# A fused Perceiver layer in eight blocks: four token buffers in place of a store and reload of the residual, and another plan for the first block

## The reference

```python
def xattn(x, ctx):                       # ctx: 257 keys of 256 for each sequence
    q, k, v = x @ Wq.T + bq, ctx @ Wk.T + bk, ctx @ Wv.T + bv
    p = softmax((q @ k.T) / sqrt(256))
    return (x + p @ v) @ Wo.T + bo
def mixer(x):                            # inner width 512, 16 states
    h = conv3(x @ in_w.T + in_b)         # depthwise over the 32 tokens
    u = silu(h)
    d, Bm = (u @ x_proj_w.T + x_proj_b)[..., :64], (...)[..., 64:]
    delta = softplus(d @ dt_w.T + dt_b)
    s[t] = exp(delta[t] * A) * s[t-1] + delta[t] * u[t] * Bm[t]     # scan over t
    return (s.sum(-1) + u * D) @ out_w.T + out_b
def ffn(x):                              # weights ternary, activations to 8 bits
    return down(silu(gate(quant(x))) * up(quant(x)))
x = x + xattn(layernorm(x), ctx)
x = x + mixer(layernorm(x))
x = x + ffn(layernorm(x))
```

## Time and profile before

| | us |
|---|---|
| median of 3 runs (lowest, highest) | 1072.03 (1071.34, 1080.11) |
| the profiled execution, its own time | 1073.63 |
| its span (first to last instruction) | 1071.8 |
| busy: PE / DVE / POOL / ACT | 950.8 / 895.7 / 858.0 / 759.6 |

### The profile page before, as it was taken

The page is one execution under the profiler, slowest core; times in us unless marked ns, Lnnn a source line. Parts: engine busy times, 40 slices in busy tenths (PEclk is TensorE's granted clock), DMA queues, the critical chain, the costliest instruction groups (busy, mean ns, idle before and its releaser), DMA issues.

```text
span 1071.8 us, 13076 instructions
## 1 busy us (share of the span) xinstructions
PE 950.8 (89%) x4175; PEld 511.9 (48%) x4210; DVE 895.7 (84%) x1210; ACT 759.6 (71%) x1321; POOL 858.0 (80%) x617
## 2 busy tenths in 40 slices
PE   8786998899988998899898998899898998687886
PEld 7452443445445554545445554446354554432554
DVE  2434797899988999799988999799987999899955
ACT  2346558777797869777796869777896869765634
POOL 1357998998978898799978898799978898899900
PEclk9997999999999999999999999999998999989999
DMA  9813440435042520535042520544042400400000
GB/s 347 323 44 158 166 169 30 168 114 221 21 143 98 214 80 21 197 129 207 20 162 91 202 79 21 197 155 180 2 177 75 143 1 2 177 0 1 1 20 20
DMA packets 21483, 122.63 MB, mean 114 GB/s; under 512 B 3431, under 2 KB 4071, under 8 KB 8872
## 3 DMA queue, kind: packets, MB, share of 16 engines
q1 hardware_dynamic: 15800, 86.99, 22.3%
q10 hardware_dynamic: 5616, 34.81, 8.7%
HBM read 114.19 MB, written 7.60 MB: 114 GB/s over the span
## 4 chain that ended last, share of the span: by engine, by line
PE 35%; ACT 22%; DVE 20%; issue 10%; DMA 6%; POOL 5%; SPq 1%; ACTq 0%; DVEq 0%; POOLq 0%
PE bank L1014 17%; PE acc L1014 13%; DVE state L877 11%; ACT decay L665 6%; DMA out<-res 3%; POOL state L598 2%; ACT u L756 2%; ACT soft L651 2%; ACT L665 2%; ACT u L764 2%; DVE raw L860 2%; ACT hid L682 2%; DMA res<-x_scratch 1%; DVE hm L943 1%; DMA brep<-in_w_gateT 1%
## 5 line engine op out<-in xcount | busy, mean ns | idle before, releaser
L877 DVE TENSOR_TENSOR_SCAN state<-decay,state 128x512 f32<-128x512 f32 (+1 forms) x352 | 590.1, 1694 | 45.5 <-ACT decay L665 27.9
L598 POOL TENSOR_TENSOR state<-w,brep 128x512 f32<-128x512 f32 (+1 forms) x352 | 612.6, 1771 | 0.1
L1014 PE MATMUL acc<-state,ident 128*128 128x512 f32 x832 | 409.2, 608 | 16.4 <-DVE state L877 12.0
L665 ACT ACTIVATE decay<-delta,neg_a 128x496 f32<-128x496 f32 x512 | 329.5, 669 | 98.6 <-DVE state L877 97.2
L1014 PEld LDWEIGHTS acc<-state,ident 128*128 128x128 f32 x832 | 147.8, 192 | 166.0 <-issue 114.2
L606 POOL TENSOR_TENSOR state<-state 128x512 f32<-128x512 f32 x96 | 122.2, 1273 | 52.6 <-DVE state L877 51.3
L651 ACT ACTIVATE soft<-x_in,nmr,rstd 128x256 f32<-128x256 f32 x64 | 33.2, 589 | 48.9 <-POOL nmr L564 48.9
L1014 PE MATMUL bank<-xn_t,in_w 128*128 128x512 f32 x128 | 60.1, 603 | 7.5 <-DVE u L1006 5.7
L629 POOL TENSOR_TENSOR w<-delta,u 128x512 f32<-128x512 f32 x32 | 39.9, 1271 | 31.0 <-ACT delta L788 31.0
L692 ACT ACTIVATE sg<-bank,ag 128x512 f32<-128x512 f32 x64 | 43.6, 681 | 29.3 <-PE bank L1014 29.0
L1014 PE MATMUL bank<-out_w,u 128*128 128x256 f32 x256 | 58.0, 382 | 6.7 <-DVE u L868 6.7
(11 more groups left out here) (145 smaller groups left out, 1348.6 us busy)
## 6 DMA issues: line engine op xcount, KB each, us to landing
keys<-in_keys_t SPq DMA_DIRECT2D x32, 1028.0 KB, 4.8
keys<-in_keys_n SPq DMA_DIRECT2D x32, 1024.0 KB
brep<-b_scratch ACTq DMA_DIRECT2D x32, 1024.0 KB, 6.7
x_in<-in_x SPq DMA_DIRECT2D x7, 512.0 KB, 5.4
x_scratch<-x_in SPq DMA_DIRECT2D x6, 512.0 KB, 2.6
res<-x_scratch SPq DMA_DIRECT2D x6, 512.0 KB, 3.5
out<-res SPq DMA_DIRECT2D x6, 512.0 KB, 8.6
brep<-in_w_gateT SPq DMA_DIRECT2D x1, 1024.0 KB, 13.4
```

What stands on the lines that cost most here:

```text
L598: nc.gpsimd.tensor_tensor(state[g % CPT][:, 0:count, :], w[:, m, :].unsqueeze(1).to_broadcast((P, count, TOK)), brep[:, n:n + count, :], A ...
L665: last = nc.scalar.activation(decay[:, to + i, :, 1:LEN], d, ACT.Exp, scale=neg_a[:, m, n + i:n + i + 1])
L877: nc.vector.tensor_tensor_scan(flat, decay[:, of:of + count, :, :].rearrange("p c q l -> p (c q l)"), flat, 0.0, ALU.mult, ALU.add).then_i ...
L1014: return nc.tensor.matmul(o, l, r, start=first, stop=last)
```

## The change

- `x_in` has four buffers; block b lives in `x_in[b % 4]` until it is stored. `res`, `x1_scratch`, the store at L528, the load at L511 and their semaphores are gone. `x2`, `stats3`, `xn3` and `finish` use `x_in[b % 4]`. The load of block j+1 waits, from j = 3 on, for the store of block j-3.
- Loads of x and stores of out go in pairs of groups: two DMAs of 256 KB where there was one of 512 KB (the first load of x excepted).
- In block 0 the keys have six buffers: the three, and `u[1]`, `w` and `delta`, which are not in use yet. SP issues six key loads, then the mixer's weights, then the last two key loads (each after the score that frees its buffer), then the feed-forward weights, then the last key rows of groups 2 and 3.
- In block 0 attention alternates between banks D, E and A, B, so the score of group g waits for the exponential of group g-2, not g-1.
- Phase 0 has its own tables (`FIRST`, and another `PREPARE`), phase 1 too (`SECOND`). Phases 2 to 7 keep their order on every engine. In phases 8 and 9 a few entries swap places.
- `softplus0` comes ahead of the `b_load`s in phase 0, and `softplus1` ahead of `c0`.
- `SIZES` makes the block sizes a table; all are 4 groups, so tiles and instruction shapes stay as they were.

Orders in phase 0 after the change. DVE: `stats1, qk, vo_rep, s_max0, s_max1, s_neg0, s_bias0, s_neg1, mixer_weights, s_bias1, s_max2, s_neg2, s_max3, s_bias2, vo_evac, s_neg3, s_bias3, p_sum0-2, abs_sum0, abs_sum1, p_sum3, abs_sum2, abs_sum3, scales, x1, ...`. PE: `turn1, query, score0, score1, vo, score2, p_turn0, score3, attend0, p_turn1, attend1, z_turn0, p_turn2, z_turn1, p_turn3, attend2, attend3, z_turn2, total, z_turn3, attn_out, ...`. ACT: `xn1, evac1, q_evac, exp0, p_last0, exp1, p_evac0, p_last1, exp2, p_evac1, exp3, p_last2, mixer_weights, z_evac0, z_evac1, zt_evac0, p_evac2, zt_evac1, p_last3, p_evac3, z_evac2, z_evac3, zt_evac2, zt_evac3, ..., x_dbl, softplus0, b_load0-3, softplus1, c0`. POOL ends with `times_u0-3, c0, c1, c2`.

```diff
-KEY_LOADS = (("t", 0), ("t", 1), ("n", 0), ("t", 2), ("n", 1), ("t", 3), ("n", 2), ("n", 3))
+FIRST_KEYS = ((("t", 0), 0), (("t", 1), 1), (("n", 0), 3), (("t", 2), 2), (("n", 1), 4), (("n", 2), 5),
+              (("t", 3), 0), (("n", 3), 1))
...
-        x_in = [sb(f"x_in{i}", [P, GROUPS, DIM]) for i in range(2)]
-        res = sb("res", [P, GROUPS, DIM])
+        x_in = [sb(f"x_in{i}", [P, GROUPS, DIM]) for i in range(4)]
...
+        keys = [sb(f"keys{i}", [P, GSEQ * HALVES * KEYS]) for i in range(3)] + [
+            k[:, :, :].rearrange("p m t -> p (m t)") for k in (u[1], w, delta)]
...
+        def att_banks(g, scan):
+            return (D, E) if scan or g % 2 == 0 else (A, B)
...
-                if post and pre:
-                    reach(sp, out_stored, j - 2, 0)
-                    sp.dma_start(res[:, :, :], t["x1_scratch"][j - 2]).then_inc(res_loaded, 16)
                 if pre:
                     if not scan:
-                        for k in range(3):
-                            load_keys(j, k)
+                        for k in range(6):
+                            load_keys(0, k)
                         load_mixer_weights()
+                        for k in (6, 7):
+                            load_keys(0, k)
                         load_ffn_weights()
...
-                    if j < BLOCKS - 2:
-                        reach(sp, res_biased[1], j, 1)
-                        sp.dma_start(t["x1_scratch"][j], x_in[par][:, :, :]).then_inc(x1_stored, 16)
...
-                    sp.dma_start(out[j - 2], (res if pre else x_in[par])[:, :, :]).then_inc(out_stored, 16)
+                    for of, at, to in pairs(b):
+                        sp.dma_start(out[at][:, to, :], x_in[b % 4][:, of, :]).then_inc(out_stored, 16)
...
                     elif part == "x2":
                         reach(dve, mixed, b, g + 1)
-                        if g == 0 and pre:
-                            reach(dve, res_loaded, b, 16)
-                        if g == 0 and not pre:
+                        if g == 0:
                             reach(dve, res_biased[1], b, 1)
...
 # LAST (phase 9): among others
-    ("h_scale", [37, 42, 59, 65]),
+    ("h_scale", [37, 42, 59, 68]),
-    ("gate", [22, 24, 25, 37, 43, 46, 58, 60]),
+    ("gate", [22, 24, 25, 37, 43, 46, 61, 63]),
```

More of the change, by code:

```diff
@@ L17 @@
 SLOTS = TILES * CPT
+SIZES = (4,) * 8
+COUNT = len(SIZES)
+FIRST_GROUP = [sum(SIZES[:b]) for b in range(COUNT + 1)]
 BG = 4
@@ new lines @@
+POST = [
+    ("h_evac", [32, 35, 73, 79]),
+    ("down", [32, 60, 75, 82]),
+    ("y_last", [0]),
+    ("x_evac", [13]),
+    ("scale_x", [12]),
+    ("tanh", [14, 16, 19, 24, 41, 46, 58, 68]),
+    ("x_max", [9]),
+    ("out_proj", [2, 2]),
+    ("x2", [4, 5]),
+    ("h_turn", [29, 33, 72, 78]),
+    ("scale_h", [21, 33, 69, 75]),
+    ("h_max", [19, 31, 54, 71]),
+    ("x_turn", [7]),
+    ("stats3", [6]),
+    ("h_floor", [20, 31, 58, 72]),
+    ("gate", [15, 17, 19, 28, 43, 45, 57, 68]),
+    ("h_scale", [22, 32, 67, 73]),
+    ("hidden", [16, 18, 20, 30, 43, 50, 63, 69]),
+    ("up", [10, 14, 17, 23, 37, 44, 51, 65]),
+    ("rstd3", [4]),
+    ("xn3", [9]),
+    ("finish", [31, 63, 77, 86]),
+]
@@ L137 @@
 }
-PREPARE = [
-    ("qk", [2]),
-    ("total", [33]),
-    ("scales", [39]),
-    ("vo_evac", [23]),
-    ("mixer_weights", [23]),
-    ("quantise", [26, 48, 63, 67]),
-    ("abs_sum", [12, 16, 22, 38]),
-    ("vo", [5]),
-    ("vo_rep", [5]),
-]
 def _scan_slots():
```

705 lines of the change are left out of this document (462 added, 243 removed).

## The result

The kernel after takes 1048.4 us (median of 4 runs, 1047.18 to 1049.7), the kernel before in the same session 1071.7: ratio 0.9749, 95% interval [0.9715, 0.9782]. Of the profiled executions before took 1073.63 us (span 1071.8), after 1048.12 (span 1046.3), so the two traces differ by 25.5 us, which is what has to be placed. The kernel before ran again in four later sessions, with medians of 1074.1 to 1075.7 us, and the kernel after once more in the last of these, with 1047.94 for 1075.52, 27.6 us less. The ratio is computed from the single executions and is not the quotient of the medians, which is 0.9783 in the first session and 0.9744 in the last; the gain is 2.2 to 2.6% by all of them.

What follows compares the result with a forecast made beforehand. It took waits shared by PE, DVE and ACT, including the residual's round trip, as the bound, with POOL in phase 1. 11.0 + 1.7 + 0.3 + 1.45 + 0.5 + 0.4 = 15.4 us won gave 1056.5 us, range 1050 to 1066.

Steps and rivals of the forecast that it cites:

- Term 1: Phases 3 to 7: DVE's five waits for the residual's reload at `x2` go, 11.0 us won (9.5 to 11.6).
- That agreement is my reason to count nearly all of it: Phases 3 to 6 less their waits, 117.5 us each, match phase 2's 117.73, which had no such wait.
- Term 2: Block 0's attention: `attn_out` 1.7 us earlier, at 48.2 for 49.89, and 0.3 more up to `x_dbl`.
- The three new waits: Block 0: `mixer_weights` ahead of `s_bias1`, `score3` of `attend0`, `total` of the last `z_turn`; gain kept small, -5 to +1.
- Term 3: End of phase 0: first scan 0.9 us later relative to `x_dbl`, but POOL's `c3` 1.45 us earlier, counted as won.
- Term 4: Phase 1's new order: same instructions in other places, 0.5 us won; at most 6.8 won or 2.6 lost.
- Term 5: Phases 8 and 9: `h_scale2` ahead of `gate6` wins 0.7 us, the split last store costs 0.33; net 0.4 won.
- The estimate of 2.3 us more: Loads and stores in halves: 512 KB would take 2.3 us longer at 138 GB/s, making the sum 1058.5.
- What was to be seen: Profile after: no DMA wait at `x2`, phases 3 to 6 at 117.5 to 117.8, `attn_out` at 48, phase 1 106 to 108 us.
- The wait is given back: Rival, phases 3 to 7: PE might set the pace, so only 4.4 us remain, 1067.6 us; chance 0.08.
- The starved start: Rival, block 0: at 203 GB/s `attn_out` comes at about 63.9, PE runs at 1.2 GHz, 1087 us; chance 0.05.

Runs made afterwards that it cites:

- r1_kept: The kernel before with four buffers of tokens and no store and reload of the residual, old tables and start kept: 1056.24 us, ratio 0.9808.
- r2_traffic: The kernel before with four token buffers, the tokens' store and a DRAM-to-DRAM read still issued, no engine waiting for the read: 1057.49 us, ratio 0.9821.
- r9_old_table0: The kernel after with phase 0 ordered by the two tables of the kernel before, six key buffers and four attention banks kept: 1067.97 us, ratio 0.9938.
- r10_old_end0: The kernel after with four rows of its first table (softplus, times_u, b_load, dt) back at or near their old places: 1051.86 us, ratio 0.9786.
- r8_old_table1: The kernel after with phase 1 ordered by the table that the kernel before used in all phases: 1054.53 us, ratio 0.9807.
- r11: The kernel after with phases 8 and 9 ordered by the tables of the kernel before: 1049.32 us, ratio 0.9766.

## Why the prediction was right and wrong

**Term 1, the reload: right about the wait, without the clock behind it.** Forecast 11.0 (9.5 to 11.6). Measured: 18.0 in phases 3 to 7, all of it from the residual (r1_kept). Of this 11.6 is the removed wait, and that nothing else would hold DVE there next was right. The other 6.4 us are what the wait did to TensorE, idle for 2.47 us and then at half clock, and the sum had no term for it: I asked only whether time comes back, and took the wait's own 11.6 as the most that could go. The step that failed is "That agreement is my reason to count nearly all of it": I set phases 3 to 6 less their waits, 117.5, beside phase 2's 117.73 and took phase 2 as the length of a phase with no wait. It was a disturbed phase itself; undisturbed is 116.4 to 116.5. Both sides had an excess, of 1.0 us from the clock behind the wait and of 1.3 from a fall of the clock that other executions do not have, and they agreed by accident. One sign was in the rows: the granted clock is 0.99 and not 1.00 in phase 2 and in phases 3 to 6, and I did not ask where the missing hundredth was. Together with phase 2, 19.3 us for 11.0. That the stores and loads themselves cost nothing was right as far as r2_traffic can show it.

**Term 2, block 0's attention: right, a little small.** Forecast 1.7 + 0.3, measured 2.5 at `attn_out` and 3.0 at `x_dbl`. The mixer's weights landed at 28.75 for the 30.0 forecast, the gate at 36.2 for 38.7, so the DMA kept the pace; `total` was not waited for at all, `attn_out` at 47.4 for 48.2. Over all executions `x_dbl` came at 78.8 to 79.7 in the eight with the new start and at 81.3 to 83.1 in the five with the old one, so the 3.0 of the two traces is typical. The three new waits that I named as the danger stayed short: DVE 2.48 us for the mixer's weights, PE 1.8 for a key load, none at `total`. r9_old_table0 has another one that I did not price: with the old order the old wait for the gate grows from 7.1 to 18.1 us, because three more key loads go ahead of it, so the new order is what makes the six buffers usable at all.

**Term 3, the end of phase 0: right.** `c3` relative to `x_dbl` came 1.7 us earlier, forecast 1.45, and the first scan 0.8 us later, forecast 0.9. Taken alone, the four rows of the table are worth 2.3 to 4.1 us at the end of phase 1 (r10_old_end0): behind the two more table loads TensorE stands idle for longer, and its clock is down for longer. The Trainium skill, page "ScalarE: Activation LUTs", section "What ACT_TABLE_LOAD costs", has a drain on top of each load; after and r10 again show an activation 1.29 to 1.30 us behind a load's start, so this trace doesn't agree.

**Term 4, phase 1's order: the other mis-sized term.** Forecast 0.5 for want of a row; 1.4 to 3.3 by r8_old_table1, with the clock's part in it. I had bounded it by POOL's idle time, 6.8 us, and taken nearly nothing within that. Terms 2 to 4 together were 3.95 and are 6.4 by the two traces; with the old start and order block 1 began at 202.7 to 204.9 in five executions, with the new ones at 196.4 to 198.3 in eight. The two traces take one of the earliest of the old and the earliest of the new.

**Term 5, the last phases: small and of no sign.** Forecast 0.4 won, the traces differ by 0.2 the other way, and r11 can't tell the tables from no change. The last store in halves is waited for 1.8 us at the end, where the whole took 2.2. The estimate of 2.3 us more, which the prediction worked out from the page "DMA: Bandwidth & Descriptors" of the Trainium skill, section "Rules for kernel authors" (transfers of 1 MiB and more), did not come.

**What was to be seen.** No DMA wait at `x2`, `attn_out` at 47.4, the mixer's weights at 28.75, `c3` at 94.7 (named: 96) and phase 1 of 106.7 us were near what was written; phases 3 to 6 at 116.5, named as 117.5 to 117.8, were not.

**The rivals.** None held. "The wait is given back" had the sign wrong: more came than was removed. The starved start did not come in this kernel; r9 has `attn_out` at 63.1, near the 63.9 of that rival, but from another wait. The sum of 15.4 fell short of the 25.5 us between the two traces by 10.1: 7.0 in phases 3 to 7, 1.3 in phase 2, 2.4 in the start and phase 1, less 0.6 in the last phases.

**What stays open.** How long phase 1 would be with no fall of the clock at all; each filling that kept it outlasted the idle time. How the 6.4 us beyond the wait divide in the kernel before itself, since the 0.97 us was measured with a delay in the kernel after. And what decides whether the clock falls at 18 to 23 us of a phase: the same instructions in the same order had it in some executions and not in others, and no run here settles why.
